# A graph network on one core: out-degrees from the stored rows, masks of destinations on GpSimd

## The reference

```python
x = _layernorm(x + _L0_gnn_ref(x, edge_index, W, b))            # normalized by degree
x = _layernorm(x + _L1_gnn_ref(x, src, dst, ...))               # attention, 8 heads
x = _layernorm(x + _L2_gnn_ref(x, edge_index, ...))             # attention, then 3 mean layers
x = _layernorm(x + _L3_gnn_ref(x, weight, norm, src, dst, rel)) # 16 relations
```

## Time and profile before

| | us |
|---|---|
| median of 3 runs (lowest, highest) | 3809.99 (3808.7, 3810.3) |
| profiled execution, time | 3814.58 |
| profiled execution, span | 3812.8 |
| TensorE busy, share of the span | 2943.8, 77% |
| VectorE | 1841.9, 48% |
| GpSimd | 1276.3, 33% |
| ScalarE | 875.8, 23% |
| counting stage, first work to the next stage's first | 81.7 to 541.2 |

### The profile page before, as it was taken

How to read it: one execution, slowest core, us unless ns; L and a number is a source line. 1 busy time by engine, 2 the same in 40 slices (tenths; PEclk the granted TensorE clock), 3 DMA queues, 4 the chain that set the end, 5 groups by cost and what they waited for, 6 DMA issues and landing times. The chain is left out here.

```text
span 3812.8 us, 46850 instructions
## 1 busy us (share of the span) xinstructions
PE 2943.8 (77%) x13253; PEld 2097.5 (55%) x13317; DVE 1841.9 (48%) x4590; ACT 875.8 (23%) x1237; POOL 1276.3 (33%) x929
## 2 busy tenths in 40 slices
PE   1777759774666666699999969999998999655565
PEld 1345537643555544466666658989894444344443
DVE  5999852355888887533233323434344221322223
ACT  0135644220100101022222224444441222000000
POOL 2000000007777740177667720000000000477776
PEclk9999979886677678899999989999999999778777
DMA  2046768314444421212222127666861444433334
GB/s 60 18 172 221 270 238 276 113 55 146 129 135 132 128 59 42 78 59 80 80 80 72 68 96 258 199 212 196 276 193 67 142 144 138 124 105 105 105 105 123
DMA packets 325254, 504.89 MB, mean 132 GB/s; under 512 B 27225, under 2 KB 238877, under 8 KB 317005
## 3 DMA queue, kind: packets, MB, share of 16 engines
q1 hardware_dynamic: 284477, 391.28, 30.5%
q0 software_dynamic: 40672, 112.31, 10.6%
HBM read 351.56 MB, written 152.75 MB: 132 GB/s over the span
## 5 line engine op out<-in xcount | busy, mean ns | idle before, releaser
L1791 POOL DMA_INDIRECT e7got<-rel_d,rel_i x416 | 394.6, 948 | 1139.9 <-POOLq L2699 1013.4
L1911 POOL DMA_INDIRECT a_got<-feat_d,src_i x416 | 404.1, 971 | 409.5 <-POOLq L2240 283.0
L1827 PE MATMUL e7sums<-e7got,e7hot 128*128 128x256 f32 x832 | 289.6, 508 | 197.0 <-DMA e7got<-rel_d,rel_i 166.4
L1425 PE MATMUL s_aggs<-s_blk_r,high 128*128 128x512 f32 (+1 forms) x1050 | 400.8, 382 | 20.7 <-DVE low L1544 20.5
L1425 PE MATMUL s_aggs<-s_blk_r,low 128*128 128x512 f32 (+1 forms) x1050 | 389.1, 371 | 0.0
L2740 PE MATMUL q_prods<-w,q_xt 128*128 128x512 f32 x800 | 352.8, 599 | 13.4 <-ACT q_xt L2760 13.4
L1827 PEld LDWEIGHTS e7sums<-e7got,e7hot 128*128 128x128 f32 x832 | 203.0, 255 | 280.4 <-issue 243.2
L1643 POOL TENSOR_SCALAR g_absent<-g_pairs 128x3200 bf16<-128x3200 f32 x25 | 274.8, 10992 | 171.4 <-DMA g_pairs<-pairs_d 171.3
L1690 PE MATMUL g_sums<-value,g_turned 128*128 128x257 f32 x1250 | 299.0, 383 | 8.6 <-ACT g_turned L1754 8.6
L1668 PE MATMUL g_scores<-key_t,g_q 128*128 128x512 f32 (+1 forms) x700 | 280.6, 556 | 19.9 <-DMA g_q<-query_d 13.3
L1799 DVE TENSOR_SCALAR e7hot<-iota,dloc,weight 128x128 f32<-128x128 f32 x416 | 115.7, 364 | 356.6 <-PE e7sums L1827 348.1
(11 more groups left out here) (422 smaller groups left out, 4469.7 us busy)
## 6 DMA issues: line engine op xcount, KB each, us to landing
s_blk<-turned_d SPq DMA_DIRECT2D x60, 1280.0 KB, 5.9
rel_d<-q_rows SPq DMA_DIRECT2D x25, 2048.0 KB, 7.5
s_blk<-turned_d SPq DMA_DIRECT2D x45, 960.0 KB, 5.1
pairs_d<-u_rows SPq DMA_DIRECT2D x25, 1600.0 KB, 8.1
turned_d<-u_line SPq DMA_DIRECT2D x25, 1600.0 KB, 7.1
g_pairs<-pairs_d SPq DMA_DIRECT2D x25, 1600.0 KB, 6.8
t_blk<-pairs_d SPq DMA_DIRECT2D x20, 1280.0 KB, 10.0
t_blk<-pairs_d SPq DMA_DIRECT2D x15, 960.0 KB, 5.1
```

The costliest lines, as they stand in the source:

```text
L1425: last = pe.matmul(aggs[:, idx % 2, half, 0:w], feats[l][part][:, a, half * P:(half + 1) * P], blk_r[:, q % RINGS, a % GA, 0:w], start=a = ...
L1791: pool.indirect_dma_start(got[:, j % U, :], None, table, bass.IndirectOffsetOnAxis(ap=index[:, j:j + 1], axis=0)).then_inc(arrived[j % U / ...
L1827: return pe.matmul(sums[:, 0:D], hot[:, u, :], got[:, u, :], start=False, stop=False)
L1911: pool.indirect_dma_start(got[:, n % 2, s, :], None, table, bass.IndirectOffsetOnAxis(ap=k.src_i[:, j:j + 1], axis=0)).then_inc(arrived[n ...
```

## The change

The marks, the tallies and `hist` go. In their place TensorE multiplies each round's part of `rows` (now of type fp32r) with `marks`, a 128x7 block of zeros with one column of ones, into `sums`: row g of `sums` holds the column sums of round g, over all tiles. At the end they are turned upright into `deg_src`. The turning of `rows` is a product with an fp32r unit matrix in place of a transpose. The masks `hot_d` are made by GpSimd, in 416 instructions written out, which wait for `used` and count `made_d` once in four; TensorE waits for `made_d` once a group. The flag is made from the in-degrees alone.

```diff
-        rows = sb("rows", [P, NP])
+        rows = sb("rows", [P, NP], F32R)
...
-        marked = sb("marked", [EP, 2, 4, P + T], BF16)
-        hist = c.enter_context(nc.psum_tensor("u_hist", [P, 512], F32))
+        largest, flag = sb("largest", [P, 1]), sb("flag", [1, 1])
+        ident_r, marks = sb("ident_r", [P, P], F32R), sb("marks", [P, FLIPS, FLIPS], F32R)
+        given = sb("given", [FLIPS, 512])
+        sums = c.enter_context(nc.psum_tensor("u_sums", [P, 512], F32))
...
+            pool.memset(rows[:].bitcast(F32), 0.0).then_inc(cleared, 1)
+
+            for j in range(S):
+                if j % 4 == 0:
+                    pool.wait_ge(used, j + 4)
+                ins = pool.tensor_scalar(hot_d[:, j % RING, :], k.iota_b[:], k.dloc[:, j:j + 1], None, ALU.is_equal)
+                if j % 4 == 3:
+                    ins.then_inc(made_d, 1)
...
-            dve.wait_ge(ready, 4)
-
-            def marks(i, b):
-                dve.wait_ge(tallied, i + 1)
-                dve.tensor_tensor(marked[:, b, :, 0:P], k.iota_b[0:EP, :].unsqueeze(1).broadcast_to([EP, 4, P]),
-                                  cols(k.slo, i * 4, 4).unsqueeze(2).broadcast_to([EP, 4, P]), ALU.is_equal).then_inc(hot, 1)
-                dve.tensor_tensor(marked[:, b, :, P:P + T], k.iota_b[0:EP, 0:T].unsqueeze(1).broadcast_to([EP, 4, T]),
-                                  cols(k.shi, i * 4, 4).unsqueeze(2).broadcast_to([EP, 4, T]), ALU.is_equal).then_inc(hot, 1)
+            step(dve.tensor_copy(ident_r[:], k.ident[:]))
+            step(dve.tensor_copy(marks[:].rearrange("p g m -> p (g m)"), k.zero[:, 0:1].broadcast_to([P, FLIPS * FLIPS])))
+            step(dve.tensor_copy(marks[:].rearrange("p g m -> p (g m)")[:, 0:FLIPS * FLIPS:FLIPS + 1],
+                                 k.ones[:, 0:FLIPS]))
+            dve.sem_inc(marked, 1)
+            dve.wait_ge(ready, 3)
...
-                    if u % 4 == 0:
-                        if closing:
-                            closings((i * 2 + u // 4 - LOOK))
-                        marks(2 * i + u // 4, u // 4)
+                    if u % 4 == 0 and closing:
+                        closings((i * 2 + u // 4 - LOOK))
                     dve.wait_ge(used, j + 1)
-                    dve.tensor_scalar(hot_d[:, u, :], k.iota_b[:], cols(k.dloc, j, 1), None, ALU.is_equal).then_inc(made, 1)
...
+            dve.wait_ge(final, 1)
+            step(dve.tensor_copy(given[:], sums[0:FLIPS, :]))
+            dve.sem_inc(given_in, 1)
+            dve.wait_ge(upright, 1)
+            by_group = counts[:, 1, 0:4 * FLIPS].rearrange("p (a g) -> p g a", a=4)
+            step(dve.tensor_copy(k.deg_src[:, 0:4 * (FLIPS - 1)].rearrange("p (g a) -> p g a", a=4), by_group[:, 0:FLIPS - 1, :]))
+            step(dve.tensor_copy(k.deg_src[:, 4 * (FLIPS - 1):T], by_group[:, FLIPS - 1, 0:T - 4 * (FLIPS - 1)]))
...
+                w = min(4, T - 4 * g) * P
+                pe.matmul(sums[0:FLIPS, 0:w], marks[:, g, :], rows[:, 4 * g * P:4 * g * P + w], start=False, stop=False)
                 for a in range(4 * g, min(T, 4 * g + 4)):
-                    last = pe.transpose(flips[:, g % 4, (a % 4) * P:(a % 4 + 1) * P], rows[:, a * P:(a + 1) * P], k.ident[:])
+                    last = pe.matmul(flips[:, g % 4, (a % 4) * P:(a % 4 + 1) * P], rows[:, a * P:(a + 1) * P], ident_r[:],
+                                     start=True, stop=True)
                 last.then_inc(flipped, 1)
 
-            def tally(i, b):
-                pe.wait_ge(hot, 2 * i + 2)
-                for u in range(4):
-                    last = pe.matmul(hist[:, 0:T], marked[:, b, u, 0:P], marked[:, b, u, P:P + T], start=False, stop=False)
-                last.then_inc(tallied, 1)
-
             def four(i, b):
-                tally(i, b)
+                pe.wait_ge(made_d, i + 1)
...
+                if closing == T - 1:
+                    pe.wait_ge(reduced, 1)
+                    pe.wait_ge(copied, T * COPIES + COPIES)
+                    pe.transpose(counts[0:1, 0, 0:P], largest[:], k.ident[:]).then_inc(laid, 1)
+            pe.matmul(sums[0:FLIPS, :], zero[:, 0:FLIPS], zero[:, 0:512], start=False, stop=True).then_inc(final, 1)
+            pe.wait_ge(given_in, 1)
+            for a in range(4):
+                last = pe.transpose(counts[:, 1, a * FLIPS:(a + 1) * FLIPS], given[:, a * P:(a + 1) * P], k.ident[0:FLIPS, 0:FLIPS])
+            last.then_inc(upright, 1)
```

More of the change, by code:

```diff
@@ L731, in count_packed @@
         apart = sb("apart", [P, 3, THIRD], I32)
-        rows = sb("rows", [P, NP])
+        rows = sb("rows", [P, NP], F32R)
         line = sb("line", [P, 2, NP])
-        largest, flag = sb("largest", [P, 2]), sb("flag", [1, 2])
-        marked = sb("marked", [EP, 2, 4, P + T], BF16)
-        hist = c.enter_context(nc.psum_tensor("u_hist", [P, 512], F32))
+        largest, flag = sb("largest", [P, 1]), sb("flag", [1, 1])
+        ident_r, marks = sb("ident_r", [P, P], F32R), sb("marks", [P, FLIPS, FLIPS], F32R)
+        given = sb("given", [FLIPS, 512])
+        sums = c.enter_context(nc.psum_tensor("u_sums", [P, 512], F32))
         counts = c.enter_context(nc.psum_tensor("u_counts", [P, BANKS, 512], F32))
         flips = c.enter_context(nc.psum_tensor("u_flips", [P, 4, 512], F32))
-        (ready, made, used, hot, tallied, final, full, copied, parted, spread_out, linked, vstep) = (sem(n) for n in (
-            "ready", "made", "used", "hot", "tallied", "final", "full", "copied", "parted", "spread_out", "linked", "vstep"))
-        reduced, laid = sem("reduced"), sem("laid")
+        (ready, cleared, marked, made, used, final, full, copied, parted, spread_out, linked, vstep) = (sem(n) for n in (
+            "ready", "cleared", "marked", "made", "used", "final", "full", "copied", "parted", "spread_out", "linked", "vstep"))
+        reduced, laid, given_in, upright = sem("reduced"), sem("laid"), sem("given_in"), sem("upright")
+        made_d = sem("made_d")
         stored, kept = sem("stored"), [sem(f"kept{b}") for b in range(2)]
@@ L752, in _ @@
             pool.memset(hot_s[:, :, THIRD:W], 1.0).then_inc(ready, 1)
-            pool.memset(rows[:], 0.0).then_inc(ready, 1)
+            pool.memset(rows[:].bitcast(F32), 0.0).then_inc(cleared, 1)
[5 more added lines that the diff above has]
+                    ins.then_inc(made_d, 1)
         @block.vector
@@ L806, in _ @@
             take_apart(T - 1)
[L807 to L810 removed]
+            step(dve.tensor_reduce(largest[:], k.deg_dst[:], AX.X, ALU.max))
             dve.sem_inc(reduced, 1)
             dve.wait_ge(laid, 1)
[L813 to L817 removed]
+            step(dve.tensor_reduce(flag[:], counts[0:1, 0, 0:P], AX.X, ALU.max))
+            step(dve.tensor_scalar(flag[:], flag[:], 255.5, None, ALU.is_gt))
+            step(dve.tensor_copy(k.heavy[:], flag[:]))
+            dve.wait_ge(final, 1)
[5 more added lines that the diff above has]
+            step(dve.tensor_copy(k.deg_src[:, 4 * (FLIPS - 1):T], by_group[:, FLIPS - 1, 0:T - 4 * (FLIPS - 1)]))
         @block.tensor
@@ L821, in _ @@
             pe.sem_inc(used, RING)
-            pe.sem_inc(tallied, 2)
-            pe.wait_ge(ready, 4)
+            pe.wait_ge(ready, 3)
             def zeros(b):
@@ L837, in multiply @@
             def multiply(u, j):
-                pe.wait_ge(made, j * 2 + 2)
+                pe.wait_ge(made, j + 1)
                 for b in range(BANKS):
@@ L844, in _ @@
                 zeros(b)
-            pe.matmul(hist[:, 0:T], zero[0:EP, 0:P], zero[0:EP, 0:T], start=True, stop=False)
+            pe.matmul(sums[0:FLIPS, :], zero[:, 0:FLIPS], zero[:, 0:512], start=True, stop=False)
+            pe.wait_ge(marked, 1)
             def flip(closing, g):
@@ L878, in four @@
                                 flip(t, g)
-                            pe.wait_ge(made, (i * 4 + u) * 2 + 2)
+                            pe.wait_ge(made, i * 4 + u + 1)
                             for n in range(BANKS):
@@ L905, in _ @@
             act.sem_inc(parted, 3)
+            act.wait_ge(cleared, 1)
             act.sem_inc(lined, FLIPS)
@@ L948, in store @@
                 sp.sem_inc(k.passed, 1)
-                sp.dma_start(pairs_d[bass.ds(t * P, P), :], rows[:]).then_inc(stored, 16)
+                sp.dma_start(pairs_d[bass.ds(t * P, P), :], rows[:].bitcast(F32)).then_inc(stored, 16)
             def store_turned(t, b):
```

13 lines of the change are left out of this document (removed).

## The result

Before 3809.3 us, after **5039.7 us** (medians of four runs each): a ratio of 1.323, interval 1.321 to 1.325. Forecast were 3780, at most 3830. The profiled execution of the kernel after has a span of 5038.4 us, 1225.6 more than before.

A forecast was written before the change was run, and what follows sets the result against it. VectorE's rhythm was taken to bound the first two stretches of the counting stage, the store chain the third. -9.9 - 22.8 + 2.9 = -29.8 us on the profiled 3814.6 gave 3784.8, as a median 3780, range 3744 to 3830.

The forecast's parts named there:

- GpSimd's order: Counting stage: GpSimd makes the next four masks while TensorE multiplies one four; waits and preamble casts cost 0.
- The slot of 0.34 + 0.36: First two stretches: wide mask 0.34 and GpSimd mask 0.36 pass in turn, 0.70 us a slot; -9.9 and -22.8 us.
- VectorE's relief: Counting stage: VectorE loses 0.195 us a slot of marks and 0.16 of masks, keeping 0.46.
- TensorE's 0.50 to 0.54 a slot: Counting stage: TensorE's products take 0.50 us a slot, 0.50 to 0.54 with the loading of the word.
- The third stretch at 11.7 "by the store chain": Eleventh to last closing: the single buffer rows and its store hold 11.7 us a tile; gain 0.
- a sign of its being wrong: Third stretch: the forecast is wrong if its tiles leave 11.7 us.
- The sums, 1.4 us a closing, hidden: Each closing: TensorE's products summing degrees take 1.4 us, hidden beside other work except at the last closing.
- The end, +2.9: Last closing: the sums aren't hidden, as the last store waits for its lines; doubled sums, +2.9 us.
- Rival 2: Counting stage: GpSimd's mask takes all the marks gave; slot 0.88, +20.3 us, 3830, slower; chance 0.20.
- its dearest case, 3877: Counting stage: nothing of VectorE's 0.46 overlaps GpSimd's 0.54; slot 1.00, +66.9 us, 3877; a quarter of the 0.20 chance.
- Rival 1: Counting stage: GpSimd's mask hides beside VectorE and TensorE bounds; slot 0.52, -59.4 us, 3751; chance 0.21.

The follow-up runs named there:

- e1: The kernel after, with the flag again made from the smaller of the largest in-degree and largest out-degree; 3919.1 us, ratio 1.0285.
- e9: e1 with GpSimd's masks handed over one by one, TensorE waiting for each at its slot; 3846.0 us, ratio 1.0088.
- e10: e9 with GpSimd's mask over 64 of the 128 columns, leaving out edges into half of the nodes; 3820.2 us, one run.
- e3: e1 with the masks of destinations made by VectorE as before, out-degrees still from the stored rows; 3806.9 us, ratio 0.9981.
- e13: e3 with the wide mask over 520 of 1041 columns, leaving out half of the edges; third stretch 163.9 us, single run.
- e7: e3 with TensorE reading both words of its eight slots at the top of the loop; 3821.2 us, ratio 1.0024.
- e12: e3 without the products of the sums, and so without the out-degrees; 3799.4 us, ratio 0.9959.
- e5: The kernel before, with GpSimd also making 416 masks that nobody reads, paced by used; 3830.1 us, ratio 1.0048.
- e6: e1 with TensorE reading both words of its eight slots at the loop's top, ahead of the wait for made_d; 3897.5 us, ratio 1.0218.
- e11: e3 storing 800 of the 3200 columns of rows, the rest zeroed once early; third stretch 164.1 us, single run.
- e14: e11 with the wide mask of e13 on top; third stretch 158.1 us, single run.
- e16: e11 without the products of the sums; third stretch 160.9 us, single run, on a chip where the kernel before took 4134 us.

## Why the prediction was wrong

- **The flag, a term that the sum never had.** The part on the change said that the flag is made from the in-degrees alone; the prediction put no price on it. The price was 1120 us, for the second pass that it lets run. The question that would have found it was there to be asked: is the largest in-degree above 255? The trace of before has 84 slots of 128 edges for the 128 nodes of the first tile, 84 edges a node on average with the most uneven ones in it, and the flag of before was a minimum, which matters only where the two differ.
- **"GpSimd's order ... I cost these at 0."** Wrong by 73 us (e1 to e9), with the reading of the word behind the wait in it. The sentence "while TensorE multiplies one four, GpSimd makes the next" holds only if making, handing over and multiplying fit: 3.4 + 1.1 + 2.0 us and the way back are 6.6 for two fours where eight slots of 0.70 are 5.6. And a closing in the middle of a four keeps the buffers back. The two stretches with closings lost most, 37.1 and 34.9 us of e1 against e9, at a lower granted clock (0.86 and 0.83 against 0.89 and 0.93).
- **The slot of 0.34 + 0.36.** GpSimd's share was too small, and the waiting was put on VectorE. The mask takes 0.60 us by itself and 0.785 to 0.83 beside wide masks, against the 0.28 to 0.44 taken from wider instructions. The half masks of e10 tell what was missing: 64 columns fewer save 0.16 us, 2.5 ns a column and so between the 2.17 and 3.43 of the earlier trace rows, which leaves a fixed part of about 0.28 us where 0.10 at most was allowed for. The collision is there, but it is mostly GpSimd that waits: its mean mask in e9's first stretch is 0.83 us against 0.60 alone, while the wide masks' mean record is 571 ns there (550 in e3). The two overlap all the same, and the slower maker sets the slot: e9's first stretch, 69.8 us, is 0.81 a slot without the 1.6 of its start. From e9 to e3 another 39 us go.
- **VectorE's relief.** Right: its busy time fell to 44.6 us in the first stretch. But the next bound was put at TensorE's 0.50 to 0.54 a slot. In e3, with VectorE's slot at 0.62, the first stretch went at 0.68 (57.4 us for 84, the same 1.6 off), and with a lighter mask (e13, first closing 149.2) no faster: TensorE's twelve products take 2.00 us, and 0.2 to 0.9 us pass before the next twelve.
- **The third stretch at 11.7 "by the store chain".** With all masks on VectorE the number held (11.3 to 11.7 in e3 and five of the kernels made from it, but 12.6 in e7), the reason didn't: a quarter of the store left 11.7. In the kernel after the tiles took 15.4 us, which the prediction had called a sign of its being wrong.
- **The sums, 1.4 us a closing, hidden.** Mostly right: e12, without them, is 7.5 us faster than e3, if that difference is real, of 35 us of products. A round of sums and four turns takes 0.63 us at full clock in e3, where 0.23 + 4 x 0.11 = 0.67 was forecast.
- **The end, +2.9.** The size was right: from the last closing to the next stage 32.8 us before (508.36 to 541.20), 35.7 in e1 (612.57 to 648.27) and 35.6 in e3. The reason holds only in part: e12, which has no sums, still takes 34.2.
- **The rivals.** Rival 2's slot of 0.88 and its sign came true (first stretch: 0.87), by another mechanism; its dearest case, 3877, is still 42 below e1. Rival 1's sum counts 184 slots in the second stretch where the earlier trace rows have 194; with those it is -54.2 and 3756. The Trainium skill (SBUF — State Buffer, Who interferes with whom) says of a VectorE instruction in a two-port mode that whichever of it and GpSimd's starts first has the shared ports for the whole instruction and the other "fully blocks". No trace here names an instruction's mode. The mask of 4.00 us in e5 agrees that GpSimd can be held up for long. Read strictly for every pair of masks, the rule gives at least 0.60 + 0.46 us a slot, and e9 has 0.81. The "roughly line-rate" of the GPSIMD Engine Reference in the Trainium skill (4.1 Engine selection) isn't what the runs show for this small mask: VectorE has a pitch of 0.16 us for it, GpSimd 0.58.

Put together, in medians: 5039.7, less the flag 3919.1, less the fours 3846.0, less GpSimd's masks 3806.9 (e3), where the kernel before had 3809 to 3814 beside them. e3, the change without its two costly parts, is the best complete version, by 0.19%.

## What to carry to other kernels

A flag that decides between two code paths is a term of the sum like any instruction: work out its value on this input before anything else. A producer moved to another engine brings a round trip with it, and the size of its portions is part of the price; compare making + hand-over + using with the time that the ring holds, and look where a portion is torn by a rarer event. An idle engine is no free engine: take its pace from the shape at hand, beside the neighbour that it will have.

## What the runs showed of the hardware

- A GpSimd compare of 128x128 bf16 takes 0.60 us with no VectorE instruction beside it and starts 0.58 behind the last (e1), one of 128x64 takes 0.44 (e10). Beside VectorE's wide masks it is 0.785 (e6) to 0.83 (e9), and 0.53 for 128x64 (e10). In e5 it is 0.89 in the first stretch and up to 4.00 where VectorE has no gap. A GpSimd record goes on while it is held up.
- A TensorE loop of 16 slots in place of 8 came with 223 more packets on the instruction queue, gaps of 1.3 to 5.9 us ahead of nearly each four in the first stretch, and 304 us.
- In e11, e14 and e16 the filling transfers of the first stretch moved 422 to 424 GB/s at their height, and the first closing came at 162 to 167 us in place of 147; in e14 TensorE has an idle time of 6.13 us there, put down to "issue". The two came together; what TensorE waited for isn't on record.
- TensorE's granted clock was 0.95 in e3's third stretch, where TensorE was busy for 86% of the time, and 0.80 in that of the kernel after, with 75%. The same products were under way for 139 us in the one and 161 in the other. More idle time doesn't always go with a lower clock: e6's third stretch has 79% and 0.75, that of before 76% and 0.95.
